# Attention's filling steps: projections first, heads turned one group ahead of the scores

## The chip, the cores and the metric

The kernel runs on one core of one Trainium2 chip. The metric is the device time of an execution in microseconds (us), lower is better. TensorE is called PE, VectorE DVE, ScalarE ACT, GpSimd POOL and SyncE SP.

## What is computed

Tokens of 32 sequences of 256 are embedded in 192 columns, go through four layers of a gated scan, and then through one attention layer and one quantised feed-forward layer. Only the attention matters for the change:

```
h = h + attention(layernorm(h))        # 12 heads of 16, 32 sequences of 256 rows
q, k, v = rows @ w{q,k,v}.T + b ; q, k rotated (partial rope)
p = softmax(q @ k.T) ; out = (p @ v) @ wo.T + bo
h = h + feed_forward(layernorm(h))     # int8 product
```

## The kernel before

The five engines run programs of their own, joined by counting semaphores. The scan layers run first (`steps`); then attention and the feed-forward run as a pipeline over sequences (`steps2`, `step2` on each engine). Step m starts sequence m; `at(k)` is sequence m - k, and a call whose sequence does not exist does nothing. Steps 2 to 9 are written out, then comes a loop over two steps at a time, then the draining steps. In step m, PE projects sequence m - 1 to q, k and v, turns and scores the heads of m - 2, and does the transposed scores, exponentials and values of m - 4. So in steps 2 and 3, the filling steps, there is no m - 4 yet: PE has only transposes of rows (`turn_x1`), projections (`project_qk`, `project_v`), transposes of heads (`turn_heads`) and scores (`scores`).

A sequence has six groups g of two heads. For each group PE turns q and k of the heads (four transposes, line 911); ACT copies them out of PSUM (`save_heads`, lines 1306 and 1307); PE computes the scores (four products of 64 rows, line 925); DVE takes the row maxima (`maxima`, line 1691). The scores lie in one PSUM pair, which is not doubled: `scores` of a group waits for the maxima of the group in front (`max_done`) as well as for its own heads (`tr_saved`). The maxima of all six groups are turned (`turn_max`, line 966), saved (`save_max`) and placed by SP with two DMAs (line 419) into the operand of the transposed scores, which the next step does first (line 938).

Everything that PE turns or projects goes through two PSUM banks, W0 and W1: projection 0 of q and k in W0, projection 1 in W1, v in W0, the heads of groups 0 to 5 in W0, W1, W0, W1, W0, W0, the maxima in W0, the rows in both. So each user waits until the one in front has been copied out; `emptied` is that wait. Before the change the bank users alternate in a filling step: heads 0; scores 0, heads 1, projection 0; scores 1, heads 2, projection 1; scores 2, heads 3, v; scores 3, heads 4; scores 4, heads 5; and the scores of group 5 open the next step.

Step 2 (`EARLY`) also ends the scan layers: PE does `rows` of the last item, and DVE its `save_y` and `residual` (line 1624) between the copy of the first projection (`save_qk`, line 1700) and the second maxima. POOL computes the inverse deviation of the next rows (`inverse_deviation2`, lines 546 to 558), rotates q and k (`rotate`), rounds rows (`round_rows2`, line 570), and takes low parts (`low_parts`, line 590) of what ACT rounded (`high_parts`, line 1317); DVE takes the rest of the rounded rows (`rest_of_rows2`, line 1680). `turn_heads` of a sequence waits for all its parts.

Of the kernel before, what the change touches and what calls it, by code (L numbers as in the profile page):

```python
# [40 lines left out]
def wait(eng, sem, value):  # L41

    if isinstance(value, int) and value <= 0:
        return
    eng.wait_ge(sem, value)


def build(nc, tokens, embedding, pos_enc, w_uv_d, w_z_d, w_o_d, gain_d, vec_d, bout, w_qkv_d, b_qkv_d, w_out_d,
# [5 lines left out]
    ITEMS = L * NCH  # L54
# [4 lines left out]
    with ExitStack() as ctx:  # L59
# [246 lines left out]
        def item(n):  # L306

            return (n, n // NCH, n % NCH, n % 2) if 0 <= n < ITEMS else None
# [23 lines left out]

        EARLY = 2

        def steps2(eng, step):

            for m in range(EARLY, LEAD2):
                step(lambda lag, m=m: m if lag is None else seq(m - lag))
            with eng.Fori(0, (SEQ - LEAD2) // 2) as j:
                for s in range(2):  # L340
                    step(lambda lag, s=s, j=j: LEAD2 + s + 2 * j if lag is None else (
                        LEAD2 + s - lag + 2 * j, (LEAD2 + s - lag) % 2))
            for m in range(SEQ, SEQ + 7):
                step(lambda lag, m=m: m if lag is None else seq(m - lag))
# [90 lines left out]
        def _(pool):  # L435
# [208 lines left out]
            def step2(at):  # L644
                inverse_deviation2(at(None))
                rounded_there(at(None), at(0))
                if at(1) is not None:
                    rotate(at(1), 0)
                round_rows2(at(0))
                it = at(3)  # L650
                if it is not None:

                    n, s = it
                    wait(pool, v_saved, n + 1)
                    wait(pool, av_done, 3 * (n - 1))
                    nc.gpsimd.tensor_tensor(
                        v_aug[:, s, :, :, 0:DH], v_rows[:, s].rearrange("p k (h d) -> p k h d", d=DH),
                        b_qkv[:, 2 * D:3 * D].rearrange("p (h d) -> p h d", d=DH)[:, None].broadcast_to([P, 2, H, DH]),
                        ALU.add).then_inc(v_placed, 1)
                it = at(1)  # L660
                if it is not None:
                    n, s = it
                    rotate(it, 1)
                    for t in range(2):

                        wait(pool, hi_ready, 2 * n + t + 1)
                        if t == 1 and at(0) is not None:

                            wait(pool, xn1_ready, at(0)[0] + 1)
                        low_parts(s, t)  # L670
                it = at(0)
                if it is not None:
                    n, s = it
                    if at(1) is None:
                        wait(pool, xn1_ready, n + 1)
                    add_rows(n, b_out, x1_biased)
                it = at(6)
                if it is not None:
                    n, s = it
                    wait(pool, xn2_ready, n + 1)  # L680
                    add_rows(n, b_ffn, x2_biased)
# [4 lines left out]
        def _(pe):  # L686
# [394 lines left out]
            def step2(at):  # L1081
                early = isinstance(at(None), int) and at(None) == EARLY


                last = isinstance(at(None), int) and at(None) >= SEQ + 3
                ending = isinstance(at(None), int) and at(None) >= SEQ + 5
                if early:
                    rows(item(ITEMS - 1), None)
                    pe.wait_ge(v_saved, 1)

                    pe.wait_ge(inp_step, 2 * ITEMS)
                elif isinstance(at(None), int) and at(None) == EARLY + 2:
                    pe.wait_ge(x_updated, ITEMS)
                for g in range(6):
                    if g == 1:
                        emptied(at, 2, tr_saved, 6, 1)
                        turn_max(at(3))
                        turn_x1(at(1), True)
                    elif g == 5 and not last:
                        emptied(at, 5, ott_saved, 1, 1)  # L1100
                        project_o(at(5))

                    scores_t(at(4), g)
                    if g == 5 and last:
                        project_o(at(5))
                    scores(at(3) if g == 0 else at(2), (g - 1) % 6)

                    if g == 2:
                        emptied(at, 2, tr_saved, 6, 2)
                        turn_back(at(5), 0)  # L1110
                    elif g == 3:
                        emptied(at, 2, tr_saved, 6, 3)
                        turn_back(at(5), 1)
                        emptied(at, 5, ot_saved, 1, 1)
                        turn_xq(at(7))
                    elif g == 4:
                        emptied(at, 2, tr_saved, 6, 4)
                        turn_o(at(5))

                    emptied(at, *((3, tr_saved, 6, 6), (1, h1_ready, 2, 1), (1, qk_saved, 2, 1), (1, qk_saved, 2, 2),  # L1120
                                  (1, v_saved, 1, 1), (2, tr_saved, 6, 5))[g])
                    turn_heads(at(2), g)
                    if g == 0 and not last:
                        emptied(at, 8, xt_saved, 1, 1)
                    if g % 2 == 0:
                        values(at(5) if g == 0 else at(4), (g // 2 - 1) % 3)

                    if g == 0:
                        if not ending:
                            emptied(at, 8, y_ready, 1, 1)  # L1130
                        if not early:
                            turn_x1(at(1), False)
                    elif g == 1:
                        emptied(at, 3, mt_saved, 1, 1)
                        project_qk(at(1), 0)
                    elif g == 2:
                        if not last:
                            emptied(at, 5, o_ready, 2, 1)
                        project_qk(at(1), 1)
                    elif g == 3:  # L1140
                        if not last:
                            emptied(at, 5, o_ready, 2, 2)
                        project_v(at(1))
                    elif g == 5:
                        emptied(at, 5, x1_ready, 1, 1)
                        if ending:
                            emptied(at, 8, y_ready, 1, 1)
                        feed_forward(at(7))
# [4 lines left out]
        def _(act):  # L1153
# [225 lines left out]
            def step2(at):  # L1379
                early = isinstance(at(None), int) and at(None) == EARLY  # L1380
                if early:

                    act.wait_ge(v_done, 1)
                    save_x1(1, False)
                elif isinstance(at(None), int) and at(None) == EARLY + 2:
                    act.wait_ge(x_updated, ITEMS)
                for g in range(6):
                    if g == 1:
                        if at(1) is not None:
                            save_x1(at(1)[0], True)  # L1390
                        save_max(at(3))
                    if g == 4 and at(5) is not None:
                        turned(B_OTT, or_t, ott_done, at(5)[0], ott_saved)
                    exps(at(4), g)
                    save_heads(at(2), g)
                    if g == 0:
                        save_o(at(5))
                        if at(1) is not None and not early:
                            save_x1(at(1)[0], False)
                    elif g == 3:  # L1400
                        if at(7) is not None:
                            turned(B_XT.bitcast(BF16), xq_t, xt_done, at(7)[0], xt_saved)
                        high_parts(at(1), 0)
                    elif g == 4:
                        high_parts(at(1), 1)
# [4 lines left out]
        def _(dve):  # L1410
# [424 lines left out]
            def step2(at):  # L1835
# [11 lines left out]
                if norm:  # L1847
# [5 lines left out]
                    wait(dve, rstd2_ready, m)  # L1853
                    wait(dve, xn1_ready, min(m, SEQ) if isinstance(m, int) else m)
                    wait(dve, xn2_ready, m - 6)
                maxima(at(2), 0)
                if norm:
                    norm_variances(first, second)
                quantise(at(7), 2)
                save_qk(at(1), 0)  # L1860
                if early:
                    save_y(item(ITEMS - 1))
                    residual(item(ITEMS - 1))

                    dve.wait_ge(s_const, 6)
                    dve.wait_ge(s_identb, 1)
                    dve.wait_ge(x_updated, ITEMS)
                normalise(at(5), 0)
                maxima(at(2), 1)
                save_qk(at(1), 1)  # L1870
# [80 lines left out]
```

## Time and profile before

| | |
|---|---|
| median of three runs | 1570.99 us (1569.74 to 1573.64) |
| the profiled execution | 1572.42 us, its span 1570.2 us |
| PE busy | 1494.2 us (95%) |
| DVE busy | 1347.7 us (86%) |
| ACT busy | 1242.8 us (79%) |
| POOL busy | 850.5 us (54%) |
| mean granted clock of PE | 0.979 |

The span is the time from the first to the last instruction in the trace; 2.2 us of the execution lie around it. Busy time of PE is the union of its matmuls. The granted clock is 1.00 at 2.4 GHz and 0.50 at 1.2 GHz. The page cuts the span in 40 slices; the changed steps lie in that of 942 to 981 us, the one slice inside the run where the granted clock reads 7 tenths. In a timeline row, "idle before" is the engine's wait just ahead of the row and the arrow names what ended it; "issue" there means that the profile shows no releaser.

### The profile page before, as it was taken

The page shows a single profiled execution, that of the slowest core. Times are in us where ns is not written, and L with a number is a line of the kernel's source. Part 1 is how long each engine was busy: PE and PEld are TensorE (multiplying, and loading weights), DVE is VectorE, ACT ScalarE, POOL GpSimd, SP SyncE. Part 2 cuts the span into 40 slices and gives each one's busy share as a digit, 9 for nine tenths or more (in the row PEclk, how much of TensorE's full clock was granted, in tenths as well). Part 3 has the DMA queues.
Part 4 walks back from the last instruction along what each step waited for, and adds up shares of the span by engine and source line. Part 5 has one row for each costly group of instructions (what it writes and reads, how often), then busy time and mean ns, then how long its engine had stood idle before and what let it go on. Part 6 is the DMA issues. An engine that isn't in the chain of part 4 may idle for free.

```text
span 1570.2 us, 36660 instructions
## 1 busy us (share of the span) xinstructions
PE 1494.2 (95%) x11441; PEld 1212.6 (77%) x11441; DVE 1347.7 (86%) x3200; ACT 1242.8 (79%) x2686; POOL 850.5 (54%) x1400
## 2 busy tenths in 40 slices
PE   4799999999999999999999997999999999999996
PEld 3678878888888888888888886677777777777763
DVE  5899999999999999999999986688888878888764
ACT  4678879898888888888888864778878777877863
POOL 7888855453335443333333245666666666666642
PEclk9899999999999999999999997999999999999998
DMA  5634201000000000000000000000000000000000
GB/s 113 141 61 83 31 1 34 1 35 0 0 1 1 1 1 0 0 1 1 1 0 0 1 1 2 2 8 12 12 16 11 11 11 11 11 11 16 11 12 26
DMA packets 24445, 27.16 MB, mean 17 GB/s; under 512 B 3104, under 2 KB 22432, under 8 KB 24352
## 3 DMA queue, kind: packets, MB, share of 16 engines
q1 hardware_dynamic: 16672, 19.70, 4.0%
q0 software_dynamic: 7680, 6.30, 3.2%
q8 instruction: 49, 0.80, 0.2%
q14 instruction: 44, 0.36, 0.1%
HBM read 14.58 MB, written 6.29 MB: 13 GB/s over the span
## 4 chain that ended last, share of the span: by engine, by line
PE 69%; POOL 11%; ACT 8%; DVE 6%; issue 6%; DMA 0%; ACTq 0%; DVEq 0%; POOLq 0%
PE banks L723 9%; PE banks L741 7%; PE banks L986 7%; PE banks L732 6%; PE banks L954 6%; POOL x L455 5%; PE banks L911 5%; PE banks L938 5%; PE banks L925 4%; PE banks L846 3%; PE banks L814 2%; PE banks L897 2%; PE banks L1010 2%; PE banks L850 2%; PE banks L900 2%
## 5 line engine op out<-in xcount | busy, mean ns | idle before, releaser
L1691 DVE TENSOR_REDUCE mx<-banks 128x4 f32<-128x1024 f32 x192 | 234.1, 1219 | 45.5 <-PE banks L925 45.1
L1297 ACT ACTIVATE probs<-banks 128x1024 f32<-128x1024 f32 x192 | 195.8, 1020 | 85.4 <-PE banks L938 81.9
L521 POOL TENSOR_TENSOR x<-x,bo_row 128x768 f32<-128x768 f32 (+1 forms) x64 | 120.1, 1876 | 129.0 <-DVE ucr_r L1552 129.0
L723 PE MATMUL banks<-ht,w_uv 128*128 128x512 f32 x576 | 171.2, 407 | 14.2 <-ACT sv_l L1271 12.2
L497 POOL TENSOR_TENSOR lnt<-mv,const 128x4 f32<-128x4 f32 x64 | 27.2, 425 | 267.3 <-DVE mv L1517 267.3
L1543 DVE SCALAR_TENSOR_TENSOR uc_h<-u_h,vec,uc_h 128x512 f32<-128x512 f32 x192 | 154.1, 803 | 2.2 <-ACT uc_h L1204 2.2
L723 PEld LDWEIGHTS banks<-ht,w_uv 128*128 128x128 f32 x576 | 107.2, 194 | 47.8 <-issue 20.9
L723 PE MATMUL banks<-ht,w_uv_rest 128*128 128x512 f32 x384 | 121.4, 398 | 0.0
L938 PE MATMUL banks<-q_t,k_t 64*128 64x256 f32 x768 | 109.3, 336 | 7.4 <-ACT probs L1297 5.9
L1543 DVE SCALAR_TENSOR_TENSOR uc_l<-u_l,vec,uc_l 128x256 f32<-128x256 f32 x192 | 104.1, 542 | 7.8 <-issue 2.9
L1526 DVE SCALAR_TENSOR_TENSOR xs<-x,rstd,xs 128x192 fp32r<-128x192 f32 x256 | 93.6, 425 | 18.3 <-ACT xs L1248 18.3
L911 PE MATMUL banks<-identr,parts 128*128 128x128 f32 x768 | 104.4, 260 | 4.0 <-issue 3.1
L1183 ACT ACTIVATE u_l<-banks,vec 64x256 f32<-64x256 f32 x128 | 60.1, 469 | 59.6 <-PE banks L723 58.8
L1248 ACT ACTIVATE xs<-x,rstd 128x192 fp32r<-128x192 f32 (+1 forms) x256 | 95.6, 459 | 13.0 <-POOL rstd L509 13.0
L1238 ACT ACTIVATE ht<-banks 128x512 fp32r<-128x512 f32 x192 | 100.8, 598 | 4.9 <-PE banks L814 3.7
L954 PE MATMUL banks<-probs,v_aug 128*32 128x256 f32 x1536 | 104.5, 390 | 0.0
L925 PE MATMUL banks<-k_t,q_t 64*128 64x256 f32 x768 | 94.9, 304 | 6.3 <-DVE mx L1691 2.3
L546 POOL TENSOR_TENSOR lnt<-mv,const 128x4 f32<-128x4 f32 x38 | 8.1, 214 | 170.1 <-DVE mv L1661 170.1
L938 PEld LDWEIGHTS banks<-q_t,k_t 64*128 64x128 f32 x768 | 70.2, 188 | 37.7 <-issue 24.3
L1306 ACT ACTIVATE q_t<-banks 128x256 fp32r<-128x256 f32 x192 | 72.5, 378 | 33.4 <-PE banks L911 32.0
L911 PEld LDWEIGHTS banks<-identr,parts 128*128 128x128 f32 x768 | 78.2, 142 | 26.7 <-issue 6.5
L846 PE MATMUL banks<-w_o,sv_h 128*128 128x192 f32 x512 | 98.2, 335 | 0.0
(189 smaller groups left out, 4719.3 us busy)
## 6 DMA issues: line engine op xcount, KB each, us to landing
out_dram<-y_out SPq DMA_DIRECT2D x32, 192.0 KB, 2.0
x<-pos SPq DMA_DIRECT2D x12, 384.0 KB, 4.2
raw_z<-w_z_dram SPq DMA_DIRECT2D x4, 704.0 KB, 5.5
raw_uv<-w_uv_dram SPq DMA_DIRECT2D x4, 576.0 KB, 4.0
q_t<-mx_t SPq DMA_DIRECT2D x64, 6.0 KB
emb<-w_qkv_dram SPq DMA_DIRECT2D x1, 864.0 KB, 7.5
w_o<-w_o_dram SPq DMA_DIRECT2D x1, 768.0 KB, 5.2
x<-embedding_dram,idx POOLq DMA_INDIRECT x48, 4.3
```

The costliest lines, as they stand in the source:

```text
L521: nc.gpsimd.tensor_tensor(rows, rows, bo_row[:, l, :][:, None, :].broadcast_to([P, CT, D]), ALU.add).then_inc(x_biased, 1)
L723: last = nc.tensor.matmul(out[:], w, r[:], start=(k == 0), stop=(k == len(passes) - 1))
L741: done = nc.tensor.matmul(out, w, r[:, s, q], start=False, stop=last and k == len(passes) - 1, skip_group_check=True)
L846: nc.tensor.matmul(out(k, False), sv_h[:, s, high(k)], w_o[:, l, 0, :], start=(k % 2 == 0), stop=False, skip_group_check=True)
L911: last = nc.tensor.transpose(B_HEADS[g][:, (2 * o + t) * P:(2 * o + t + 1) * P].bitcast(F32R), parts[:, s, t, o, 2 * g:2 * g + 2, :].rearr ...
L925: last = nc.tensor.matmul(B_S[j][:, t * S:(t + 1) * S], q_t[q, s, g, t * P:(t + 1) * P], k_t[q, s, g, :], start=True, stop=True)
L938: last = nc.tensor.matmul(B_ST[j][:, t * S:(t + 1) * S], k_t[q, s, g, t * P:(t + 1) * P], q_t[q, s, g, :], start=True, stop=True)
L954: last = nc.tensor.matmul(bank[32 * h:32 * h + 32, c:c + S], v_aug[:, s, t, 4 * p + h, :], probs[:, (s + p) % 2, h // 2, (2 * (h % 2) + t) ...
L986: last = nc.tensor.matmul(dst, h1_t[:, t_, g_, :], w, start=(k == 0), stop=(k == len(passes) - 1))
L1297: act.activation(probs[:, (s + g // 2) % 2, g % 2, :].rearrange("p (j k) -> p j k", j=2), B_SST, ACT.Exp, scale=float(DH) ** -0.5).then_in ...
L1543: nc.vector.scalar_tensor_tensor(out=uc, in0=uk, scalar=v(l, part, V_W0 + k), in1=uc, op0=ALU.mult, op1=ALU.add).then_inc(taps, 1)
L1691: nc.vector.tensor_reduce(mx[:, s].rearrange("p t (j h) -> p j t h", j=2)[:, :, :, g], B_SS.rearrange("p j (t k) -> p j t k", t=2), AX, AL ...
```

## The change

Steps 2 and 3 (`filling`) get an order of their own on PE, ACT, DVE and POOL. All instructions stay the same in kind and number.

- PE: first the rows of the next sequence, then the scores of group 5 left over from the step in front, then both projections and v; then heads 0; and from there on heads g are turned before the scores of g - 1. `turn_max` goes from ahead of group 0's scores to behind those of group 2.
- DVE: the variances come first, then (step 2) `save_y` and `residual`, then the copies of the three projections, then the maxima, with `rest_of_rows2` between the second and the third.
- ACT: both copies of the turned rows first, then the copies of the heads; `high_parts` of tile 0 stays behind group 3, of tile 1 goes behind group 5; `save_max` goes behind group 3.
- POOL: `round_rows2` comes ahead of the first `rotate`.

```diff
--- before.py
+++ after.py
@@ -332,6 +332,10 @@
 
         EARLY = 2
 
+        def filling(m):
+
+            return isinstance(m, int) and EARLY <= m < EARLY + 2
+
         def steps2(eng, step):
 
             for m in range(EARLY, LEAD2):
@@ -644,9 +648,14 @@
             def step2(at):
                 inverse_deviation2(at(None))
                 rounded_there(at(None), at(0))
-                if at(1) is not None:
+                if filling(at(None)):
+                    round_rows2(at(0))
                     rotate(at(1), 0)
-                round_rows2(at(0))
+                elif at(1) is not None:
+                    rotate(at(1), 0)
+                    round_rows2(at(0))
+                else:
+                    round_rows2(at(0))
                 it = at(3)
                 if it is not None:
 
@@ -1091,6 +1100,32 @@
                     pe.wait_ge(inp_step, 2 * ITEMS)
                 elif isinstance(at(None), int) and at(None) == EARLY + 2:
                     pe.wait_ge(x_updated, ITEMS)
+                if filling(at(None)):
+
+
+                    if not early:
+                        emptied(at, 3, tr_saved, 6, 6)
+                        turn_x1(at(1), False)
+                    turn_x1(at(1), True)
+                    scores(at(3), 5)
+                    project_qk(at(1), 0)
+                    project_qk(at(1), 1)
+                    emptied(at, 1, qk_saved, 2, 1)
+                    project_v(at(1))
+                    emptied(at, 1, v_saved, 1, 1)
+                    turn_heads(at(2), 0)
+                    emptied(at, 1, qk_saved, 2, 2)
+                    for g in range(1, 6):
+
+                        if g == 5:
+                            emptied(at, 2, tr_saved, 6, 5)
+                        if g == 4:
+                            emptied(at, 3, mt_saved, 1, 1)
+                        turn_heads(at(2), g)
+                        scores(at(2), g - 1)
+                        if g == 3:
+                            turn_max(at(3))
+                    return
                 for g in range(6):
                     if g == 1:
                         emptied(at, 2, tr_saved, 6, 1)
@@ -1384,6 +1419,17 @@
                     save_x1(1, False)
                 elif isinstance(at(None), int) and at(None) == EARLY + 2:
                     act.wait_ge(x_updated, ITEMS)
+                if filling(at(None)):
+                    if not early:
+                        save_x1(at(1)[0], False)
+                    save_x1(at(1)[0], True)
+                    for g in range(6):
+                        save_heads(at(2), g)
+                        if g == 3:
+                            save_max(at(3))
+                            high_parts(at(1), 0)
+                    high_parts(at(1), 1)
+                    return
                 for g in range(6):
                     if g == 1:
                         if at(1) is not None:
@@ -1853,18 +1899,30 @@
                     wait(dve, rstd2_ready, m)
                     wait(dve, xn1_ready, min(m, SEQ) if isinstance(m, int) else m)
                     wait(dve, xn2_ready, m - 6)
+                if filling(m):
+                    norm_variances(first, second)
+                    if early:
+                        save_y(item(ITEMS - 1))
+                        residual(item(ITEMS - 1))
+
+                        dve.wait_ge(s_const, 6)
+                        dve.wait_ge(s_identb, 1)
+                        dve.wait_ge(x_updated, ITEMS)
+                    save_qk(at(1), 0)
+                    save_qk(at(1), 1)
+                    save_v(at(1))
+                    maxima(at(2), 0)
+                    maxima(at(2), 1)
+                    rest_of_rows2(m, first)
+                    maxima(at(2), 2)
+                    maxima(at(2), 3)
+                    maxima(at(2), 4)
+                    return
                 maxima(at(2), 0)
                 if norm:
                     norm_variances(first, second)
                 quantise(at(7), 2)
                 save_qk(at(1), 0)
-                if early:
-                    save_y(item(ITEMS - 1))
-                    residual(item(ITEMS - 1))
-
-                    dve.wait_ge(s_const, 6)
-                    dve.wait_ge(s_identb, 1)
-                    dve.wait_ge(x_updated, ITEMS)
                 normalise(at(5), 0)
                 maxima(at(2), 1)
                 save_qk(at(1), 1)
```

## Rows read from the trace of the kernel before

**Rows 1.** Windows by stage: length, busy of PE, PEld, DVE, ACT, POOL, granted clock, DMA.
```profile
942.80:958.60 15.80, 10.53 (x66) 8.29 (x66) 10.46 (x18) 6.35 (x21) 10.41 (x23) 0.81 0.01 2
958.60:975.00 16.40, 13.47 (x80) 10.51 (x80) 10.98 (x15) 7.09 (x23) 10.87 (x22) 0.71 0.00 1
```

**Rows 2.** Timeline of PE in step 2: start, length, line, tiles, count, idle before.
```profile
942.28 0.51 PE L858 MATMUL banks<-ones,hc_l 64*128 64x1 f32 x8
943.45 0.51 PE L911 MATMUL banks<-identr,parts 128*128 128x128 f32 x4 [0.67 <-POOL parts L590]
...
945.84 1.29 PE L986 MATMUL banks<-w_qkv,h_t 128*128 128x384 f32 x3
946.92 0.84 PE L986 MATMUL banks<-w_qkv_rest,h_t 128*128 128x384 f32 x2
...
948.99 0.83 PE L986 MATMUL banks<-w_qkv,h_t 128*128 128x384 f32 x3
949.66 0.51 PE L986 MATMUL banks<-w_qkv_rest,h_t 128*128 128x384 f32 x2
951.56 0.50 PE L925 MATMUL banks<-k_t,q_t 64*128 64x256 f32 x4 [1.40 <-DVE mx L1691]
...
952.37 0.55 PE L986 MATMUL banks<-w_qkv,h_t 128*128 128x192 f32 x3
...
953.31 0.38 PE L986 MATMUL banks<-w_qkv_rest,h_t 128*128 128x192 f32 x2
...
956.41 0.80 PE L925 MATMUL banks<-k_t,q_t 64*128 64x256 f32 x4 [0.75 <-ACT k_t L1307]
957.14 0.75 PE L911 MATMUL banks<-identr,parts 128*128 128x128 f32 x4
958.64 0.80 PE L925 MATMUL banks<-k_t,q_t 64*128 64x256 f32 x4 [0.75 <-ACT k_t L1307]
```

**Rows 3.** Timeline of DVE in step 2.
```profile
948.60 1.40 DVE L1624 SCALAR_TENSOR_TENSOR x<-banks,ysb,x 128x192 f32<-128x192 f32 x4
950.19 1.23 DVE L1691 TENSOR_REDUCE mx<-banks 128x4 f32<-128x1024 f32 x1 [0.20 <-DVE x L1624]
...
952.10 1.23 DVE L1691 TENSOR_REDUCE mx<-banks 128x4 f32<-128x1024 f32 x1 [0.22 <-PE banks L925]
953.24 1.34 DVE L1680 SCALAR_TENSOR_TENSOR xs<-x,rstd,xs 128x192 fp32r<-128x192 f32 x2
954.50 0.54 DVE L1709 COPY v_rows<-banks 128x384 f32<-128x384 f32 x1
...
957.25 1.23 DVE L1691 TENSOR_REDUCE mx<-banks 128x4 f32<-128x1024 f32 x1 [1.07 <-PE banks L925]
```

**Rows 4.** Timeline of ACT: the copy of turned keys, and the first exponential's table.
```profile
958.21 0.38 ACT L1307 ACTIVATE k_t<-banks 128x256 fp32r<-128x256 f32 x1
...
975.09 1.28 ACT L1297 ACT_TABLE_LOAD   x1
```

**Rows 5.** Windows of two microseconds, columns as in Rows 1.
```profile
949.00:951.00 2.00, 1.17 (x7) 0.85 (x5) 1.80 (x5) 0.66 (x2) 1.73 (x6) 0.96 0.00 0
...
955.00:957.00 2.00, 1.10 (x8) 0.90 (x8) 1.18 (x2) 1.30 (x5) 0.59 (x2) 0.74 0.04 8
...
961.00:963.00 2.00, 2.00 (x13) 1.58 (x12) 0.71 (x3) 0.94 (x3) 0.00 (x0) 0.50 0.00 0
...
965.00:967.00 2.00, 2.00 (x13) 1.69 (x13) 1.67 (x2) 0.66 (x2) 1.53 (x7) 0.70 0.00 0
```

**Rows 6.** Timeline of PE at the head of step 4.
```profile
974.21 0.79 PE L938 MATMUL banks<-q_t,k_t 64*128 64x256 f32 x4
...
978.01 0.59 PE L966 MATMUL banks<-ident,mx 128*12 128x128 f32 x2 [1.00 <-ACT k_t L1307]
```

**Rows 7.** Timeline of POOL in step 2.
```profile
947.10 0.21 POOL L546 TENSOR_TENSOR lnt<-mv,const 128x4 f32<-128x4 f32 x1 [2.83 <-DVE mv L1661]
```

**Rows 8.** The page's DMA issues: count, KB each, us from issue to landing.
```profile
out_dram<-y_out SPq DMA_DIRECT2D x32, 192.0 KB, 2.0
```

## The prediction, made before the changed kernel ran

> **What bounds the kernel now.** Over the whole span PE is busy 95%, so what counts is what PE waits for in the steps that change. I read three views in this order. The windows by stage give the two filling steps 15.8 and 16.4 us, with PE busy 10.5 and 13.5 and a granted clock of 0.81 and 0.71 [rows 1]: 8.2 us of PE idle and some time lost to the low clock, in 32.2 us of 1570. That is all there is to win here. The timelines then show what PE waits for. Scores of one group start 2.23 us apart at the end of step 2 (956.41 and 958.64) [rows 2]. Between them lie scores (0.80), turn (0.75), ACT's copy of the heads to 958.59 [rows 4], and the trace names ACT as the releaser. But the maxima of the group in front run from 957.25 to 958.48 [rows 3], and `scores` waits for them too; DVE's release takes 0.14 (maxima end 951.42, scores start 951.56 [rows 2, 3]), so they would have released PE at 958.62. The two waits end within 0.05 us of each other. This is the row that decides my forecast: turning the heads ahead takes away the wait that is named and leaves one equally long. Third, the windows of two microseconds show where the clock is low [rows 5].
>
> **The change part by part.** Times are of the profiled execution. I follow when PE starts each set of scores.
>
> *Cadence of the groups.* With heads ready, a group costs scores, maxima and two releases: 1.91 us at full clock (maxima at 950.19 and 952.10 [rows 3]); at the low clock scores take 0.80 instead of 0.50 [rows 2], so 2.23. Bounds: no less than 1.23, the maxima alone; no more than 2.23 plus the 0.05. I take these rows, since nothing in them is extrapolated. `rest_of_rows2` now lies behind the second maxima. It took 1.34 beside a working POOL [rows 3]; I take 0.75, as POOL then waits for ACT, between bounds of 0.6 and 1.4. The scores of group 2 (0.80 and releases) run beside it, so it costs nothing with its cover and 0.6 if it is the long one.
>
> *Projections first.* The projection of q and k of one tile takes 1.18 at full clock (948.99 to 950.17) and 1.92 at the low one (945.84 to 947.76); v takes 1.32 (952.37 to 953.69) [rows 2]. Together 3.68 at full clock, and by the ratio 1.63 an estimated 6.0 at the low one. Before, each projection lay beside the maxima of a group, so DVE covered it; now DVE has no maxima to do meanwhile, only copies. Behind them comes a chain that was also hidden: the copy of v 0.54 with releases 0.72 [rows 3], the first turn 0.51 [rows 2], ACT's copy of both halves with releases 0.74 [rows 2, 4]: 1.97.
>
> *Step 2.* PE's last product of the scan layers ends at 942.79 [rows 2]. Before, PE waited 0.67 for POOL's parts and turned heads 0 at 943.45; that wait goes. Now: two turned rows and ACT's copy of them, 0.36 + 0.38 (the same size as in [rows 4]) + 0.09 of releases, give 943.62; projections, 947.30; I take them at full clock, though the one at 945.84 was low, since PE now idles 0.5 us ahead of them and not 0.67 and 0.75 us in two gaps, and has dense work from 943.6 on; chain 1.97, so scores 0 at 949.27. `save_y` and `residual` (0.2 + 1.40 [rows 3]) run on DVE beside the projections and free the second maxima, which they delayed before; if they lost that cover they would cost at most 1.6. Then 1.91 to scores 1; from there to scores 3 two maxima, the rest of the rows between, and releases: 0.84 + 1.23 + 0.75 + 1.23 + 0.14 = 4.19; then 2 x 2.23. Scores 5 start at 959.83, against 958.64: 1.2 late.
>
> *The clock.* At 1.2 GHz the scores and turns of a group leave PE idle half the time. The clock was 0.96 in 949 to 951, still full when v was projected at 952.4 to 953.7, 0.74 in 955 to 957 and 0.50 at 957: it fell some 2.3 us after the last projection. It rose about 3.3 us after the first low projection, at 949.2 (from 945.84), and at 966.2 (0.70 in 965 to 967) [rows 5]. In the new step 2 it will fall near scores 1 and stay low until the next projections. That is why four of five cadences above are slow.
>
> PE was busy for nearly all of 961 to 963, yet at 0.50 [rows 5]; what ran was turns and scores, and only from 962.9 a projection. The Trainium skill (TensorE: Matmul & The Clock Gate, Part 4: PE-mode transpose) says that a transpose does not count as PE activity in the way a matmul does. By it, turns set close together do nothing for the clock, which speaks against an order that parts them from the projections: the groups run low, as in the sum. Did turns count like products, the sum would be the first rival's below. The row agrees with the page.
>
> *Step 3.* Scores 5 end at 960.63 and the projections start, low for 3.3 us (55% of 6.0), then full for 1.7: 965.6. Chain 1.97: first scores at 967.6. Cadences 1.91 + 4.19 + 2.23: scores 4 at 975.9, end 976.7. There step 4 begins with its transposed scores, which started at 974.21 [rows 6]: 2.4 us late.
>
> *What else moves.* `turn_max` goes behind group 2, some 4 us ahead of the transposed scores; ACT's copy and SP's two DMAs must fit in. This trace has no landing for them; SP's 192 KB DMAs landed in 2.0 us [rows 8], and they are far smaller. I take 0; bounds 0 and 1. POOL waited 2.83 us for the variances [rows 7], which now come first, so its inverse deviation starts up to 2.8 us earlier and the moved `round_rows2` (under 1 us in front of `rotate`) is covered. `high_parts` of tile 1 behind group 5 makes POOL's last parts late: in step 3 ACT ends the heads near 976.0, the high parts 1.1 later, low parts 1.2 later: 978.3, and step 4's first turn comes at about 978.8. Cover 0.5 us; bounds 0 to 1. Queued behind ACT's high parts is the exponential, which needs the transposed scores anyway.
>
> *Step 4 on.* Before, ACT's table load began at 975.09 [rows 4], once the transposed scores were there, and PE waited at 978.01 for what followed it [rows 6]; the whole shifts with them. PE is busy for 95% of the run, so I take it that nothing behind gives the 2.4 back or adds to it. Sum: 1572.42 + 2.4 = 1574.8 for an execution like the profiled one. That one lies 1.4 above the median of the runs, so the forecast of the median is 1573.4 us, slower by 0.15%.
>
> **The rivals.** (a) The clock stays up: the step is then 3 x 0.3 + 0.7 shorter in step 2 and 2.3 + 1.3 shorter in step 3, about 4 in all: 1.6 faster than before, 1569.4; with all small bounds at their good ends 1568. For it: projections in one block are the densest work these steps have. Against: some 10 us of half-idle PE lie between two blocks, and less sufficed for the fall at 956. (b) The slower side: the clock falls ahead of the first block (before, the projection at 945.84 ran low [rows 2]), and does not rise in the second before it ends. The first block costs 2.3 more and its cadences 0.3, the second 1.9 more; 2.4 + 4.5 = 6.9: 1577.9. It decides if the granted clock is 0.5 during step 2's projections. For: PE still idles about 0.5 us in front of them. Against: more dense work follows than before. (c) The change does what it says: the copy of the heads cost PE more than the 0.05 us that I read, through the turn and scores queued behind it. For it: the trace names ACT as the releaser. Against: with one PSUM pair for the scores, 0.50 + 1.23 and two releases still stand between them. Eight cadences at 0.1 to 0.4 less give 1 to 3 back: 2 off the forecast, 1571.4, no change at all.
>
> **How the numbers follow.** Forecast 0.45, (a) 0.22, (b) 0.13, (c) 0.20. A measurement of this kernel can tell about 0.3%, 4.7 us, from no change (the three runs spread over 3.9). Inside it lie the forecast, (a), (c), so same 0.83; slower by more needs (b) or the forecast with its bad bounds: 0.12; faster by more would need half of all PE's idle time: 0.05. Range: from (a) 1569.2 to short of (b), 1576.8.
>
> **What would show it.** Right: in steps 2 and 3 the projections stand in a block with DVE idle; behind it maxima start 1.9 apart, or about 2.2 where the clock is 0.5, each released by PE, and PE's scores by `mx`, not by `k_t`; the first transposed scores start 1 to 4 us later than 974.2, and step 4 onward takes what it took. Wrong: scores closer than 1.9, a full clock through the groups, a wait of PE for `parts` or of the transposed scores for the DMA, or a different length of the loop's steps.

## The result: slower by 0.57%

The changed kernel takes 1583.67 us (median of 8 runs, 1579.64 to 1588.39), the kernel before beside it 1572.72; the ratio is 1.0057 with a 95% interval of 1.0039 to 1.0074, so 9.0 us more (6.1 to 11.6). The two medians lie 11.0 apart; one execution of the kernel before took 1990.01 us and is not in the ratio. The forecast was 1573.4 in a range up to 1576.8.

One moment divides the profile well: the end of PE's last product of the scan layers (942.79 in [rows 2], 945.43 after). From there to the fifth turning of maxima, in step 7, I call the filling. It took 88.81 us before and 95.09 after: 6.28 more. From the fifth to the thirtieth turning both need the same, 456.91 and 456.90.

**The profile after.** Windows of steps 2 and 3, columns as in [rows 1]:

```profile
945.43:961.84 16.41, 11.04 (x73) 8.75 (x73) 10.07 (x16) 6.93 (x23) 10.35 (x23) 0.78 0.01 1
961.84:984.73 22.89, 15.34 (x74) 12.37 (x75) 10.34 (x15) 7.17 (x23) 10.62 (x22) 0.57 0.00 1
```

Step 2 is 0.6 us longer than before when both are counted from the scan layers' end (16.41 against 15.85); step 3 went from 16.4 to 22.9, with PE idle 7.6 us of it and the clock at 0.57. The timeline of PE answers to [rows 2] and [rows 6]. Line numbers are those of each run's own kernel: 920, 934, 947 and 995 here are 911, 925, 938 and 986 before.

```profile
949.07 0.39 PE L995 MATMUL banks<-w_qkv_rest,h_t 128*128 128x192 f32 x2
950.11 0.88 PE L920 MATMUL banks<-identr,parts 128*128 128x128 f32 x8 [0.65 <-DVE v_rows L1755]
951.39 0.50 PE L934 MATMUL banks<-k_t,q_t 64*128 64x256 f32 x4 [0.41 <-ACT k_t L1342]
951.82 0.54 PE L920 MATMUL banks<-identr,parts 128*128 128x128 f32 x4
953.30 0.50 PE L934 MATMUL banks<-k_t,q_t 64*128 64x256 f32 x4 [0.95 <-DVE mx L1737]
...
961.84 0.80 PE L934 MATMUL banks<-k_t,q_t 64*128 64x256 f32 x4 [0.48 <-DVE mx L1737]
962.57 1.33 PE L995 MATMUL banks<-w_qkv,h_t 128*128 128x384 f32 x3
...
967.58 0.63 PE L995 MATMUL banks<-w_qkv_rest,h_t 128*128 128x192 f32 x2
971.93 1.26 PE L920 MATMUL banks<-identr,parts 128*128 128x128 f32 x8 [3.72 <-DVE v_rows L1755]
973.43 0.80 PE L934 MATMUL banks<-k_t,q_t 64*128 64x256 f32 x4 [0.24 <-ACT k_t L1342]
...
983.09 0.66 PE L947 MATMUL banks<-q_t,k_t 64*128 64x256 f32 x4
```

Behind v's projection PE waits 0.65 us for its copy in step 2, and 3.72 in step 3. DVE's timeline of step 3 names what DVE waited for, and POOL's shows where that stood:

```profile
966.17 0.56 DVE L1746 TENSOR_TENSOR qk_rows<-banks,b_qkv 128x384 f32<-128x384 f32 x1 [0.95 <-PE banks L995]
971.32 0.56 DVE L1755 COPY v_rows<-banks 128x384 f32<-128x384 f32 x1 [4.59 <-POOL v_aug L665]
974.27 1.23 DVE L1737 TENSOR_REDUCE mx<-banks 128x4 f32<-128x1024 f32 x1 [2.40 <-PE banks L934]
```

```profile
964.85 0.20 POOL L550 TENSOR_TENSOR lnt<-mv,const 128x4 f32<-128x4 f32 x1 [2.08 <-DVE mv L1707]
...
967.62 0.83 POOL L574 TENSOR_TENSOR xs<-x,rstd 128x384 fp32r<-128x384 f32 x1
968.41 0.65 POOL L584 TENSOR_TENSOR rot<-qk_rows,rope 128x96 f32<-128x96 f32 x2
...
970.23 0.99 POOL L665 TENSOR_TENSOR v_aug<-v_rows,b_qkv 128x384 f32<-128x384 f32 x1
```

`save_v` of sequence 2 writes into the buffer that held sequence 0 and so waits for `v_placed` of sequence 0, which POOL does in the same step 3, behind the inverse deviation, the rounding and the first rotate. These three stood ahead of the placing before, too. What moved is the copy. Before, v was projected behind the heads of group 3, and its copy started after the placing had ended:

```profile
969.53 1.55 DVE L1680 SCALAR_TENSOR_TENSOR xs<-x,rstd,xs 128x192 fp32r<-128x192 f32 x2 [0.55 <-POOL xs L570]
971.00 0.54 DVE L1709 COPY v_rows<-banks 128x384 f32<-128x384 f32 x1
```

```profile
969.45 1.00 POOL L656 TENSOR_TENSOR v_aug<-v_rows,b_qkv 128x384 f32<-128x384 f32 x1
```

Now v is projected ahead of all heads. Counted from the scan layers' end, DVE copied v at 28.2 us before; now PE has it ready at 22.8, and POOL starts the placing only at 24.8 (26.7 before).

### The profile page after: what moved, and what is told of

Same layout as the page of the kernel before. It is cut to its first block, busy times and chain, and to the rows that moved or that the text cites. A ratio compares the mean times of both kernels' runs of the same rounds, so it can differ in the third digit from the quotient of the medians.

```text
span 1583.5 us, 36652 instructions
## 1 busy us (share of the span) xinstructions
PE 1506.6 (95%) x11441; PEld 1223.5 (77%) x11441; DVE 1348.1 (85%) x3200; ACT 1241.1 (78%) x2686; POOL 850.2 (54%) x1400
## 4 chain that ended last, share of the span: by engine, by line
PE 75%; ACT 8%; DVE 8%; issue 4%; POOL 1%; ACTq 0%; DVEq 0%; POOLq 0%
PE banks L732 10%; PE banks L750 9%; PE banks L995 7%; PE banks L741 7%; PE banks L963 6%; PE banks L920 5%; PE banks L947 5%; PE banks L934 4%; PE banks L855 4%; PE banks L823 3%; PE banks L859 2%; PE banks L906 2%; PE banks L1019 2%; PE banks L909 2%; PE banks L863 2%
## 5 line engine op out<-in xcount | busy, mean ns | idle before, releaser
L501 POOL TENSOR_TENSOR lnt<-mv,const 128x4 f32<-128x4 f32 x64 | 27.2, 426 | 267.9 <-DVE mv L1563 267.9
L594 POOL TENSOR_TENSOR parts<-qk_rows,parts 128x192 fp32r<-128x192 f32 x128 | 73.8, 597 | 56.0 <-ACT parts L1352 55.9
```

## The experiments

The ratio is to the kernel before, run beside each. The other columns are from the profiles, in us from the scan layers' end: the start of the last scores of sequence 0 (end of step 2), of the first scores of sequence 1, of the first transposed scores, and the length of the filling.

| | ratio, interval | last of step 2 | first of seq. 1 | transposed | filling |
|---|---|---|---|---|---|
| before | | 15.85 | 18.86 | 31.42 | 88.81 |
| e5, before again | 0.9991 (0.9975 to 1.0008) | 14.97 | 17.97 | 30.12 | 87.32 |
| changed | 1.0057 (1.0039 to 1.0074) | 16.41 | 28.00 | 37.66 | 95.09 |
| e4, changed again | 1.0062 (1.0038 to 1.0086) | 16.42 | 28.01 | 37.67 | 95.07 |
| e1, values first | 1.0021 (1.0000 to 1.0042) | 16.41 | 23.47 | 32.54 | 89.95 |
| e9, own buffer | 0.9998 (0.9985 to 1.0012) | 16.70 | 23.83 | 32.90 | 90.56 |
| e7, values ahead of rotate | 1.0033 (1.0015 to 1.0052) | 16.40 | 25.98 | 35.37 | 93.02 |
| e2, step 2 only | 1.0004 (0.9987 to 1.0021) | 16.39 | 19.40 | 32.06 | 89.57 |
| e3, heads behind | 1.0097 (1.0073 to 1.0121) | 19.42 | 31.07 | 41.65 | 100.18 |
| e8, filler products | 0.9998 (0.9977 to 1.0019) | 15.52 | 21.95 | 33.94 | 91.55 |
| e6, copy first | 0.9984 (0.9967 to 1.0001) | 17.03 | 20.04 | 30.52 | 87.26 |
| e10, copy first again | 0.9980 (0.9968 to 0.9993) | 16.32 | 19.32 | 31.02 | 87.47 |

Theory V says that the loss is the wait of v's copy; theory S that it is the serial block of projections and the low clock; theory U that it lies outside the filling.

**e1: values first.** `place_values` holds the old call, which stood where its second call stands now; `...` marks what is left out.

```diff
             def step2(at):
+                first_values = isinstance(at(None), int) and at(None) == EARLY + 1
+                if first_values:
+                    place_values(at(3))
                 inverse_deviation2(at(None))
...
+                if not first_values:
+                    place_values(at(3))
```

> The changed kernel with one call moved on POOL: in step 3 the values of sequence 0 are placed first, ahead of the inverse deviation, the rounding and the first rotate. Theory V (the loss is the wait of v's copy for POOL: in step 3 PE stood idle 3.72 us until 971.93, DVE 4.59 us until POOL had placed the values): the idle goes, the first scores of step 3 come 3.2 to 3.7 us earlier, and from the end of the scan layers' last product to the loop's steps the kernel is 3 to 5 us shorter, about half of the 6.3 us lost there; the whole 4 us faster than the changed kernel. Theory S (the loss is that the projections stand in a block with nothing beside them and the groups run at the low clock): the wait is replaced by another of the same length, under 1 us gained. Theory U (the loss lies ahead of and behind attention's filling): no more than 1 us either.

PE's idle ahead of step 3's first turn fell from 3.72 to 0.65 us:

```profile
962.86 0.38 PE L1001 MATMUL banks<-w_qkv_rest,h_t 128*128 128x192 f32 x2
963.89 0.88 PE L926 MATMUL banks<-identr,parts 128*128 128x128 f32 x8 [0.65 <-DVE v_rows L1761]
965.18 0.50 PE L940 MATMUL banks<-k_t,q_t 64*128 64x256 f32 x4 [0.41 <-ACT k_t L1348]
```

The scores came 4.5 us earlier, above the 3.2 to 3.7 expected: 3.1 us of it is the wait, and most of the rest the clock, since the projections' second half ran at the full clock in this profile (0.38 in the first row against 0.63 for the same products in the changed kernel). The filling is 5.1 us shorter, just above the 3 to 5 expected, and by the ratios the whole is 5.7 us faster than the changed kernel. What is left of the filling's loss is 1.1 us against the first profile of before and 2.6 against the second. Theory V holds for most of the loss; theory S may have the rest, which no run isolates.

**e9: the same wait taken away in another way.** POOL's order stays.

```diff
+        v_first = sb("v_first", [P, 2, D])
...
-                wait(dve, v_placed, n - 1)
+                if not (isinstance(n, int) and n == 2):
+                    wait(dve, v_placed, n - 1)
...   # save_v and the placing use v_first for sequence 0
```

> The changed kernel, every engine's order as it is, but the rows of v of sequence 0 have a buffer of their own, so that the copy of v of sequence 2 has nothing to wait for on POOL. Theory V in its narrow form (PE's idle of 3.7 us is the reuse of that buffer and nothing else): DVE copies v as soon as PE has it, the first scores of step 3 start 23.5 us after the scan layers' end as with the values first, though POOL still places them at its old, late place; the filling is 1 to 2 us longer than before and not 6.3. If POOL's late values held up something else too, the number stays above 25.

```profile
968.75 0.56 DVE L1760 COPY v_rows<-banks 128x384 f32<-128x384 f32 x1 [0.54 <-PE banks L998]
```

```profile
971.94 1.00 POOL L666 TENSOR_TENSOR v_aug<-v_first,b_qkv 128x384 f32<-128x384 f32 x1
```

DVE copies v 3.2 us before POOL starts to place the values of sequence 0. The first scores came at 23.83, and the filling at 90.56, which is 1.75 us longer than the first profile of before: as expected. It is the reuse of the buffer and nothing else that POOL's late values held up.

**e7: half the dose.** `place_values` stands behind `round_rows2` and ahead of the rotate in step 3.

> A dose between the changed kernel and the one with the values first: in step 3 POOL places the values behind the rounding and ahead of the first rotate. Theory V: v's copy comes earlier by the rotate's 1.8 us, PE's idle ahead of step 3's first turn falls from 3.7 to about 1.9 us, and the first scores of step 3 start 26.2 us after the scan layers' end, between 28.0 (changed) and 23.5 (values first). If the wait were for something else that came with the move, the number would be that of one of the two.

```profile
966.62 0.56 DVE L1761 COPY v_rows<-banks 128x384 f32<-128x384 f32 x1 [2.78 <-POOL v_aug L654]
```

```profile
967.23 0.89 PE L926 MATMUL banks<-identr,parts 128*128 128x128 f32 x8 [1.91 <-DVE v_rows L1761]
```

PE was idle for 1.91 us where 1.9 was expected, and the scores came at 25.98 where 26.2 was. Moving the values past the rotate is worth the rotate.

**e2: the new order in step 2 alone.**

```diff
-            return isinstance(m, int) and EARLY <= m < EARLY + 2
+            return isinstance(m, int) and m == EARLY
```

> Only step 2 has the new order, step 3 the old one. In the profile of the changed kernel step 2 ended 0.6 us later than before, counted from the last product of the scan layers. Theory V: nearly all of the loss lies in step 3, so that the loss there falls from 6.3 us to between 0 and 1.5 and the whole is 5 us faster than the changed kernel. Theory S: both steps lose alike, and half of the loss, 3 us, stays.

The filling is 0.76 us longer than in the first profile of before and 2.3 longer than in the second, and the ratio, 1.0004, does not tell the kernel from before. So the new order costs little in step 2, and step 3 carries the loss.

**e3: heads behind the scores, projections still first.**

```diff
-                        turn_heads(at(2), g)
                         scores(at(2), g - 1)
+                        turn_heads(at(2), g)
                         if g == 3:
+                            emptied(at, 2, tr_saved, 6, 3)
                             turn_max(at(3))
```

The added wait is for heads that the scores just ahead of it have already waited for.

> The changed kernel with the heads of a group turned behind the scores of the group in front again, projections still first. If, as the prediction held, scores wait for the maxima of the group in front as long as for the heads, this changes a group's cadence by no more than 0.1 us (1.9 at the full clock, 2.2 at the low one), under 1 us in all. If turning the heads ahead is what the change gains, each of ten groups gets 0.3 to 0.7 us longer, 3 to 7 us.

The filling got 5.1 us longer than the changed kernel's. That lies in the 3 to 7 of the second expectation, but the groups did not get longer as it said. The timeline of PE shows where the time went.

```profile
943.40 1.28 PE L995 MATMUL banks<-w_qkv,h_t 128*128 128x384 f32 x3 [0.47 <-ACT h_t L1324]
...
954.36 0.80 PE L934 MATMUL banks<-k_t,q_t 64*128 64x256 f32 x4 [0.75 <-ACT k_t L1343]
955.09 0.74 PE L920 MATMUL banks<-identr,parts 128*128 128x128 f32 x4
956.63 0.80 PE L934 MATMUL banks<-k_t,q_t 64*128 64x256 f32 x4 [0.80 <-ACT k_t L1343]
...
959.62 0.75 PE L920 MATMUL banks<-identr,parts 128*128 128x128 f32 x4
961.12 1.00 PE L988 MATMUL banks<-identr,xs 128*128 128x128 f32 x6 [0.75 <-ACT k_t L1343]
962.05 0.80 PE L934 MATMUL banks<-k_t,q_t 64*128 64x256 f32 x4
```

Here most of the first block of projections ran at the low clock (1.28 against 0.79 for its first row), which the changed kernel escaped in both profiles: 1.5 us to the first scores, with the same instructions ahead of them. From group to group at the low clock the scores start 2.22 to 2.27 us apart, against 2.20 to 2.22 with the heads ahead: about 0.05, as predicted. But heads 5 behind the scores end the step with nothing beside them: ACT's copy (0.75) and the turned rows (six transposes) now stand ahead of the last scores, 3.15 us instead of 2.21, and heads 5 of step 3 stand ahead of the transposed scores, 1.40 instead of 0.56. So turning ahead gains at the ends of the steps, 1.8 us in all, which my rival (c) had in the wrong place. Up to the transposed scores e3 is 4.0 us behind the changed kernel; another 1.1 is lost in step 4, where its first heads wait 1.51 us for POOL's parts.

**e8: what the low clock costs.** On top of e1.

```diff
                         scores(at(2), g - 1)
+                        for _ in range(2):
+                            nc.tensor.matmul(B_OT2[:], identr[:], w_qkv[:, 0, 0:512], start=True, stop=True)
```

> The kernel with the values first, and behind each group's scores in steps 2 and 3 two products of 128 x 512 that nobody reads, ten pairs in all, into a bank that is free then (the result is not touched). They fill PE's idle time and measure what the low clock costs. If the low clock in the groups is the larger part of theory S, the granted clock stays near 1.00 in both steps and in step 4, the cadence of the scores goes from 2.2 to 1.9 us, the second block of projections from about 5 to 3.7 us, and the filling becomes 3 to 5 us shorter than with the values first, 2 to 4 shorter than before. If it is only the serial order, the fillers cost PE 0.4 us a group that it had idle, and nothing changes, or it gets up to 2 us longer.

Windows of the two steps of e8:

```profile
948.73:964.25 15.52, 11.88 (x83) 9.31 (x84) 10.07 (x16) 6.67 (x22) 9.79 (x22) 1.00 0.00 1
964.25:982.70 18.45, 16.14 (x82) 11.42 (x82) 10.09 (x15) 6.55 (x23) 10.31 (x23) 0.70 0.00 1
```

In step 2 it did what was hoped: clock 1.00 (0.80 in e1), scores 1.91 us apart throughout, 0.9 us gained, and 0.6 in the next block, which waited 0.61 us for a copy of DVE now. Then the clock fell in step 3 all the same, behind the first scores. From its start to the start of the next row a pair of fillers took 0.57 us of PE at the full clock and takes 1.02 there:

```profile
973.32 1.22 PE L1133 MATMUL banks<-w_qkv,identr 128*128 128x512 f32 x2
974.34 0.67 PE L926 MATMUL banks<-identr,parts 128*128 128x128 f32 x4
```

PE has no idle time left ahead of most scores, and these now start 2.3 to 3.5 us apart. The filling is 1.6 us longer than e1's, inside the "up to 2 us longer" of the other expectation. The profiled execution was the slowest of e8's twelve (1585.33 us; they lie between 1567.03 and 1585.33), and the ratio, 0.9998, is not above e1's 1.0021. So the profile shows a gain in step 2 and a loss in step 3, and the runs show no clear gain or loss of the whole against e1.

**e4 and e5: the two kernels again.**

> The changed kernel unchanged, for a second profile. In the first, the scan layers ended 2.6 us later than before and the steps behind the loop took 4.4 us longer, with a low clock in them, though neither has a changed instruction. If these belong to the change (theory U), they come again, within 0.5 us. If they are chance, they fall anywhere between 0 and 5 us, while the loss in the filling steps, 6.3 us, comes again within 1 us.

> The kernel before, unchanged. In both profiles of the changed kernel the scan layers ended 2.6 and 3.7 us later than in the first profile of before, in the three other variants 0.2 to 1.1 us earlier. If that is chance, this second profile of before can fall anywhere in that spread (941.7 to 946.5 us); if it belongs to the changed program alone, it ends them at 942 to 943 us. The filling steps come again within 0.5 us, and the ratio to before is 1.000 within its interval, which shows how much of a difference such a comparison tells.

The filling of the changed kernel comes again to 0.02 us. That of before comes again only to 1.5, where I had expected 0.5; 0.9 of it lies in step 2, where the granted clock was 0.84 and not 0.81. The scan layers ended at 945.43 and 946.48 in the two profiles of the changed kernel, at 942.79 and 944.27 in those of before, and over all twelve profiles between 941.7 and 948.7, e8 being the latest with the same scan layers. From the thirtieth turning to the span's end the twelve took 78.8 to 86.1 us, e1 80.3 and the changed kernel 86.1 and 82.2. This end follows the granted clock: 78.8 us where its mean was 0.94 (e6, e10), 79.9 to 82.2 where it was 0.89 to 0.92, 84.5 at 0.83 (e7), 86.0 at 0.82 (e8 and the first profile of the changed kernel). So these parts scatter by more than what they were suspected of, and theory U finds no support. If U were right, I had put before's second scan end at 942 to 943; at 944.27 it speaks for chance.

**e6 and e10: a use of what was learned, in the old order.** The edit below holds in steps 2 and 3 only, and POOL has e1's move besides. Both runs are the same kernel.

```diff
                 maxima(at(2), 2)
-                rest_of_rows2(m, first)
                 save_v(at(1))
...
                 maxima(at(2), 3)
+                rest_of_rows2(m, first)
```

> The kernel before with its old order on PE and ACT, and two moves in steps 2 and 3: DVE copies v ahead of the rest of the rounded rows, which goes behind the fourth maxima, and POOL places the values of sequence 0 first in step 3. In the old order PE waited 1.02 and 1.58 us for the copy of v. Theory V (copies that free a bank must not stand behind POOL's work): both waits shrink to under 0.5 us, and the filling becomes 1 to 2 us shorter than before. Theory S and every theory in which the maxima pace these groups: the wait moves to the maxima and under 0.5 us is gained.

> The old order with the two moves (v copied first, values of sequence 0 placed first) again, for a second profile: the first one had a low clock through the second half of step 2, which made it 1.2 to 2.1 us longer than in the two profiles of before, and a step 3 of 13.5 us against 15.6 and 15.2. If the clock was chance, step 2 now ends 14.5 to 16 us after the scan layers, and step 3 again takes 13 to 14; the filling comes to 85.5 to 87.5 us against 88.8 and 87.3.

In e6 PE's wait for v's copy was gone in step 2 (1.02 us before) and went from 1.58 us to 0.27 in step 3:

```profile
973.02 0.51 PE L917 MATMUL banks<-identr,parts 128*128 128x128 f32 x4 [0.27 <-issue]
974.28 0.50 PE L931 MATMUL banks<-k_t,q_t 64*128 64x256 f32 x4 [0.75 <-ACT k_t L1313]
```

Both profiles had the low clock through the second half of step 2 (it ended at 17.03 and 16.32, the second above what I expected), and step 3 to its transposed scores took 13.5 and 14.7 us, against 15.6 and 15.2 before; the second is above the expected 14. The filling, 87.3 and 87.5 us, is inside what I expected, but it is also that of before's better profile. The ratios are 0.9984 and 0.9980, the second with 1 outside its interval, but before against itself gave 0.9991. That the wait shrinks is shown; that the kernel is faster for it, by 0.1 to 0.2%, is suggested and not settled.

## Why the prediction was wrong

**The step that failed** is the chain behind the projections: "the copy of v 0.54 with releases 0.72". It takes DVE's copy as ready to start once PE is done. I had looked at what stands ahead of it on DVE, and not at its second wait, on POOL's placing of the sequence two before, which stands three jobs down POOL's queue in the same step. In the profile before that wait never shows, because the rest of the rows, in front of the copy on DVE, ended later: the copy started at 971.00, and POOL's placing had ended at 970.45. POOL's own move is not to blame, since the placing came 1.9 us earlier than before, counted from the scan layers' end. Up to the chain the sum was right: the second block of projections ended at 22.8 us, as forecast. The chain behind it took 5.2 us and not 1.97. e9, e1 and e7 show why: without the wait the first scores of step 3 come at 23.5 to 23.8 us, with it and one rotate less at 26.0, with all of it at 28.0. My sum had 24.8.

**The cadence and its tie** held. Scores lay 1.91 to 1.92 us apart at the full clock in step 2, 2.20 to 2.22 at the low one, where I had 1.91 and 2.23 (1.91 and the 0.30 by which scores are longer make 2.21). In step 2 the maxima released PE in the two full-clock groups and the last, and ACT's copy in the two between, where the maxima's end and release make the same time within 0.05. The rest of the rows took 0.74, where I had 0.75. At the low clock PE is idle a third of a group (0.75 of 2.23), not half, as I wrote. e3 gives 0.05 us a group for heads ahead. What I missed is that turning ahead matters at the two step ends.

**Projections first.** Step 2 was forecast 1.2 late and came 0.6 late; the first scores were forecast at 6.48 after the scan layers' end and came at 5.96 (the chain took 1.93 against my 1.97, but the three projections set close together took 3.26 where I had added 3.68 from rows read one by one). The full clock came 3.3 us after the start of the second block in my sum; in the changed kernel it came after 5.7 us, as the block ended, and the block took 5.64 where I had 5.0. v's projection, low throughout (0.63 against 0.38), is 0.9 us longer than in step 2. The start, 0.7 earlier than forecast, made up for it.

**Step 3** was forecast with 8.33 us from first to fifth scores and took 9.10, all at the low clock and with 0.26 for the wait of `turn_max`'s copy, which I had at 0. The transposed scores started at 37.66 instead of 33.9; e1, which has the change without the missed wait, at 32.5. So without the wait the forecast of 2.4 late would have been about right: in the filling e1 and e9 lose 1.1 and 1.8 us against the first profile of before, 2.6 and 3.2 against the second.

**The rivals.** The full clock (a) happened in step 2 of e8 alone, by products that the change does not have. The low first block (b) happened in e3, with the same instructions ahead of it as in the changed kernel, and cost 1.5 us there, where I had 2.3 for it. Neither is the result. The price of (a) was summed wrongly: its own terms, 1.6 in step 2 and 3.6 in step 3, make 5.2 us and not 4, so 1568.2 and not 1569.4. Of what would show me wrong, "a wait of PE for `parts`" was the nearest; the wait was for `v_rows`.

**What stays open.** The filling explains 6.3 us, or 7.0 against the mean of before's two profiles; the ratio says 9.0 with an interval from 6.1. Over the variants the ratio's difference less the filling's, against that mean, lies between -4 and +3 us, so the rest may be the scatter of the scan layers and the tail, but no run shows where it went. The window of 961 to 963 in [rows 5], which I read as turns not raising the clock, holds scores as well as turns, and no run parts the two.

## What to carry to other kernels

When a copy out of PSUM moves earlier, list every semaphore that it waits for, not only its queue: a buffer that is used again two sequences on brings in another engine's whole order. A wait that a trace never shows is hidden, not absent; for each one ask what covers it now. Before removing the wait that the profile names, look at the second that ends with it.

## What the runs showed of the hardware

PE's granted clock can be full while PE does nothing and low while it works. These are windows of two microseconds of the changed kernel in step 3:

```profile
965.00:967.00 2.00, 2.00 (x10) 2.00 (x9) 0.77 (x2) 0.00 (x0) 1.68 (x5) 0.50 0.00 0
967.00:969.00 2.00, 1.21 (x6) 0.97 (x5) 0.00 (x0) 0.00 (x0) 1.78 (x5) 0.67 0.00 0
969.00:971.00 2.00, 0.00 (x0) 0.00 (x0) 0.00 (x0) 0.00 (x0) 1.92 (x4) 1.00 0.00 0
971.00:973.00 2.00, 1.07 (x8) 1.07 (x8) 0.56 (x1) 0.28 (x1) 1.92 (x5) 0.68 0.00 0
```

The block of projections (962.57 to 968.21) ran at 1.2 GHz to its end. The full 2.4 GHz came as it ended, lay in the idle time behind it, and was gone when the first heads were turned at 971.93 (1.26 us for eight transposes, against 0.88 in step 2). The two profiles of before show the same on a smaller scale: the same instructions ended step 2 at 15.85 and at 14.97 us, with a granted clock of 0.81 and 0.84. What a few microseconds of half-idle PE cost here depends on when the clock happens to change, so one profile does not make a microsecond there an effect.
